# Weighing the values with the values as the stationary operand, in column halves, and one reduction for both heads' largest scores

## What is computed

```
q, k = rope(x @ wq.T + bq, x @ wk.T + bk)          # 16 heads of 64, 512 tokens
s = q @ k.T / sqrt(64), causal                     # per head, 512 x 512
p = exp(s - max(s))                                # kept undivided
o = (p @ v) / sum(p) + bv                          # v without its bias
out = concat(o over heads) @ wo.T + bo
```

## Time and profile before

| | us |
|---|---|
| median of 3 executions | 2499.45 (2493.75 to 2513.72) |
| the profiled execution | 2502.42 |
| its span on the core | 2500.5 |
| what lies around the span | 1.92 |

### The profile page before, as it was taken

The page is one execution under the profiler, slowest core; times in us unless marked ns, Lnnn a source line. Parts: engine busy times, 40 slices in busy tenths (PEclk is TensorE's granted clock), DMA queues, the critical chain, the costliest instruction groups (busy, mean ns, idle before and its releaser), DMA issues.

```text
span 2500.5 us, 38952 instructions
## 1 busy us (share of the span) xinstructions
PE 2057.5 (82%) x11640; PEld 1430.8 (57%) x11640; DVE 1680.5 (67%) x2937; ACT 1187.7 (47%) x2702; POOL 951.3 (38%) x581
## 2 busy tenths in 40 slices
PE   4147788998899888998889878998889988989985
PEld 1013366665567556665566556665566655666764
DVE  2975678558965798558865788558876588645431
ACT  1214366345643466345653456344663456424631
POOL 0330366106920386106930277104850077203501
PEclk9558789999999999999999989998999998999997
DMA  2000002231123212231113212231123211142233
GB/s 103 0 0 17 17 35 71 91 109 43 57 70 113 69 51 74 90 110 40 61 64 119 68 42 84 67 106 56 43 68 116 85 45 55 65 133 71 71 105 116
DMA packets 82452, 175.06 MB, mean 70 GB/s; under 512 B 11448, under 2 KB 42560, under 8 KB 81984
## 3 DMA queue, kind: packets, MB, share of 16 engines
q1 hardware_dynamic: 78144, 164.05, 19.0%
q0 software_dynamic: 4096, 8.40, 1.1%
HBM read 123.71 MB, written 15.14 MB: 56 GB/s over the span
## 4 chain that ended last, share of the span: by engine, by line
PE 50%; DVE 22%; issue 14%; ACT 6%; POOL 4%; DMA 3%; SPq 1%; DVEq 0%; ACTq 0%; POOLq 0%
PE G L1065 7%; DVE HS L1542 7%; PE G L1050 5%; PE FM L1039 3%; PE FC L1027 3%; PE G L943 3%; PE G L954 3%; PE G L937 3%; ACT REG L1347 2%; DMA MW<-moe 2%; PE G L1082 2%; PE FM L907 2%; DVE maxes L1843 2%; DVE HC L1564 2%; PE FM L749 2%
## 5 line engine op out<-in xcount | busy, mean ns | idle before, releaser
L1542 DVE TENSOR_TENSOR_SCAN HS<-DA,D 128x1024 f32<-128x1024 f32 x128 | 374.8, 2928 | 20.5 <-ACT DA L1224 19.9
L1065 PEld LDWEIGHTS G<-REG 128*128 128x128 f32 x2560 | 350.4, 199 | 60.6 <-issue 50.2
L1065 PE MATMUL G<-REG 128*128 128x64 f32 x2560 | 358.6, 273 | 3.2 <-DVE REG L1855 3.2
L1967 POOL TENSOR_TENSOR Y<-Y,HC 128x1024 f32<-128x1024 f32 x114 | 269.1, 2361 | 181.3 <-DVE HC L1564 180.3
L1050 PE MATMUL G<-ident,REG 128*128 128x128 f32 x1280 | 242.1, 289 | 116.3 <-ACT REG L1347 114.0
L1347 ACT ACTIVATE REG<-G 128x128 f32<-128x128 f32 (+3 forms) x512 | 223.4, 436 | 121.4 <-PE G L1050 117.0
L1978 POOL TENSOR_TENSOR REG<-REG,cos_t 128x512 f32<-128x512 f32 x128 | 170.4, 1331 | 264.2 <-ACT REG L1323 264.1
L1050 PEld LDWEIGHTS G<-ident,REG 128*128 128x128 f32 x1280 | 149.0, 150 | 166.1 <-issue 132.6
L1339 ACT ACTIVATE REG<-G,maxes 128x128 f32<-128x128 f32 (+3 forms) x384 | 195.6, 510 | 81.9 <-DVE maxes L1843 81.9
L1981 POOL TENSOR_TENSOR REG<-REG 128x512 f32<-128x512 f32 x128 | 204.2, 1596 | 57.4 <-DMA REG<-ROT 48.8
L1039 PE MATMUL G<-REG 64*128 64x128 f32 (+3 forms) x768 | 217.8, 481 | 8.4 <-POOL REG L1981 7.4
(11 more groups left out here) (290 smaller groups left out, 4272.4 us busy)
## 6 DMA issues: line engine op xcount, KB each, us to landing
MW<-moe SPq DMA_DIRECT2D x120, 768.0 KB, 4.2
REG<-ROT SPq DMA_DIRECT2D x256, 128.0 KB
EW<-experts SPq DMA_DIRECT2D x16, 514.5 KB, 4.7
XG<-x_rows SPq DMA_DIRECT2D x8, 960.0 KB, 5.4
y_rows<-YO SPq DMA_DIRECT2D x120, 64.0 KB, 1.5
X<-xT SPq DMA_DIRECT2D x8, 256.0 KB, 6.1
W<-weights SPq DMA_DIRECT2D x1, 2048.0 KB, 9.5
REG<-xT SPq DMA_DIRECT2D x8, 256.0 KB, 3.2
```

The source lines that it names most:

```text
L1065: mm = pe.matmul(G[3][:, col:col + DK], PT[:, n % 2, c * P:(c + 1) * P], V[:, c, j * P + h * DK:j * P + (h + 1) * DK], start=c == 0, stop= ...
L1542: dve.tensor_tensor_scan(HS[:, :, :].rearrange("p h s -> p (h s)"), DA[:, n % 2, :, :].rearrange("p h s -> p (h s)"), D1[:, :, :].rearrang ...
L1967: pool.tensor_tensor(Y[:, :, :], Y[:, :, :], HC_EARLY if early else HC[:, n % 2, :, :], ALU.add).then_inc(y_add.sem, 1)
```

## The change

`weigh_values` now takes both heads of a step together. V is the stationary operand (64 columns) and PT moves (128 columns), so the result comes out turned: head 0 on partitions 0 to 63 of G3 and head 1 on partitions 64 to 127. `turn_out` is gone. ACT copies G3 into O when a pair is done. The reciprocals can no longer be applied along partitions, so PE spreads them over the bank FC with eight small products (`spread_inverse`), and DVE multiplies O by that bank straight into the slot. The bias bv goes through wo once, at the start, and is added to bo. G1 with G0 and FM with G4 are now two tensors of two banks each, and `largest` reduces both heads of a step in one instruction. `front(0)` on POOL has a new wait.

```
...
+        SCORES = [ctx.enter_context(nc.psum_tensor(n, [P, 2, S], F32)) for n in ("G1_G0", "FM_G4")]
...
             if t_ == OUT_STEP and j_:
-                guest[s_] = (("out", j_ - 1), (ot_copy, j_))
+                guest[s_] = (("out", j_ - 1), (o_d, j_))
...
-            def weigh_values(b, n):
-                pe.wait_ge(pt_copy.sem, pt_copy.at(b, n + 1))
...
-                col = t * P + h * DK
                 for c in range(t + 1):
-                    mm = pe.matmul(G[3][:, col:col + DK], PT[:, n % 2, c * P:(c + 1) * P],
-                                   V[:, c, j * P + h * DK:j * P + (h + 1) * DK], start=c == 0, stop=c == t)
+            def weigh_values(b, s):
+                pe.wait_ge(pt_copy.sem, pt_copy.at(b, 2 * s + 2))
...
+                    for h in range(2):
+                        mm = pe.matmul(G[3][h * DK:(h + 1) * DK, t * P:(t + 1) * P], V[:, c, j * P + h * DK:j * P + (h + 1) * DK],
+                                       PT[:, h, c * P:(c + 1) * P], start=c == 0, stop=c == t)
...
+            def spread_inverse(b, j):
+                pe.wait_ge(rec_d.sem, rec_d.at(b, j + 1))
                 bank = take(b, ("out", j))
                 for t in range(TILES):
-                    mm = pe.transpose(bank[:, t * P:(t + 1) * P], O[:, t * P:(t + 1) * P], ident[:, :])
-                mm.then_inc(ot_mm.sem, 1)
+                    for h in range(2):
+                        mm = pe.matmul(bank[h * DK:(h + 1) * DK, t * P:(t + 1) * P],
+                                       rows[:, j % 2, 1, h * TILES + t:h * TILES + t + 1].to_broadcast([P, DK]), ident[:, :],
+                                       start=True, stop=True)
+                mm.then_inc(rinv_mm.sem, 1)
...
                     turn(b, 2 * s)
-                    if s:
-                        weigh_values(b, 2 * s - 1)
...
                     elif key[0] == "out":
-                        turn_out(b, key[1])
+                        spread_inverse(b, key[1])
...
-                    if t_ == 0 and s + 2 < STEPS:
+                    if s + 2 < STEPS:
                         scores(b, s + 2)
-                    weigh_values(b, 2 * s)
-                    if t_ and s + 2 < STEPS:
-                        scores(b, s + 2)
-                weigh_values(b, N_TILES - 1)
+                    weigh_values(b, s)
+                spread_inverse(b, PAIRS - 1)
                 for j in range(PAIRS - 1):
                     project_out(b, j)
-                turn_out(b, PAIRS - 1)
...
             def copy_out(b, j):
...
-                act.wait_ge(ot_mm.sem, ot_mm.at(b, j + 1))
-                act.activation(ot_slot(j), ring_bank[("out", j)][:, :], ACT.Identity, bias=vec("bv", j)).then_inc(ot_copy.sem, 1)
+                act.wait_ge(pv_mm.sem, pv_mm.at(b, PER_PAIR * (j + 1)))
+                act.activation(O, G[3][:, :], ACT.Copy).then_inc(o_copy.sem, 1)
...
                     copy_turned(b, 2 * s)
+                    if s and s % TILES == 0:
+                        copy_out(b, s // TILES - 1)
...
+            def largest(b, s):
+                dve.wait_ge(sc_mm.sem, sc_mm.at(b, 2 * s + 2))
+                dve.tensor_reduce(maxes[:, j % 2, :].rearrange("p (h t) -> p h t", h=2)[:, :, t], SCORES[s % 2][:, :, 0:(t + 1) * P], AX.X, ALU.max,
                                   negate=True).then_inc(nm_d.sem, 1)
...
+                dve.wait_ge(o_copy.sem, o_copy.at(b, j + 1))
+                dve.wait_ge(rinv_mm.sem, rinv_mm.at(b, j + 1))
+                dve.tensor_tensor(ot_slot(j), O, ring_bank["out", j][:, :], ALU.mult).then_inc(o_d.sem, 1)
...
                     if key[0] == "proj":
                         rotate(b, key[1])
+                    elif key[0] == "out":
+                        divide(b, key[1])
...
                 for n in range(STATES):
+                    if n + 1 < STATES:
+                        pool.wait_ge(scan_d.sem, scan_d.at(b, n + 2))
+                        pool.sem_inc(pool_passed, 1)
                     front_step(b, n)
```

More of the change, by code:

```diff
@@ L235, in build @@
         y_rows = nc.dram_tensor("y_rows", (MOE_TILES * MOE_ROWS, D), F32).ap()
-        FB, FC, FM = (ctx.enter_context(nc.psum_tensor(n, [P, S], F32)) for n in ("FB", "FC", "FM"))
-        G = [ctx.enter_context(nc.psum_tensor(f"G{k}", [P, S], F32)) for k in range(5)]
+        FB, FC = (ctx.enter_context(nc.psum_tensor(n, [P, S], F32)) for n in ("FB", "FC"))
+        SCORES = [ctx.enter_context(nc.psum_tensor(n, [P, 2, S], F32)) for n in ("G1_G0", "FM_G4")]
+        FM = SCORES[1][:, 0, :]
+        G = [SCORES[0][:, 1, :], SCORES[0][:, 0, :], *(ctx.enter_context(nc.psum_tensor(f"G{k}", [P, S], F32)) for k in (2, 3)), SCORES[1][:, 1, :]]
         n_loads, n_late = 16 * 10, 16 * 3
@@ L328, in build @@
         o_d = signal("o_d", PAIRS)
-        ot_mm = signal("ot_mm", PAIRS)
-        ot_copy = signal("ot_copy", PAIRS)
+        rinv_mm = signal("rinv_mm", PAIRS)
+        o_copy = signal("o_copy", PAIRS)
         wo_mm = signal("wo_mm", PAIRS)
@@ L1164, in late @@
                 pe.wait_ge(s_late, n_late)
-                pe.wait_ge(s_made, 17)
+                for j in range(PAIRS):
+                    mm = pe.matmul(G[2][:, 0:1], w("wo", j * D), vec("bv", j), start=j == 0, stop=j == PAIRS - 1)
+                mm.then_inc(s_bv, 1)
+                pe.wait_ge(s_made, 18)
             def finish(t):
@@ L1394, in phase_2 @@
                         add_bias(b, key[1])
-                    elif key[0] == "out":
-                        copy_out(b, key[1])
                     elif key[0] == "turn":
@@ L1881, in phase_2 @@
                 largest(b, 0)
-                largest(b, 1)
                 if f is not None:
@@ L1888, in phase_2 @@
                     if s + 1 < STEPS:
-                        largest(b, 2 * s + 2)
-                        largest(b, 2 * s + 3)
+                        largest(b, s + 1)
                     if t_ == 0 and j:
-                        divide(b, j - 1)
+                        invert_sums(b, j - 1)
                     if s == 1:
@@ L1923, in late @@
                 dve.tensor_scalar(q_b, q_b, DK ** -0.5, None, ALU.mult).then_inc(s_made, 1)
-                dve.wait_ge(s_made, 17)
+                dve.wait_ge(s_bv, 1)
+                dve.tensor_tensor(vec("bo"), vec("bo"), G[2][:, 0:1], ALU.add).then_inc(s_made, 1)
+                dve.wait_ge(s_made, 18)
             def finish(t):
```

56 lines of the change are left out of this document (23 added, 33 removed).

## The result

The changed kernel takes 2555.07 us (median of 4 executions, 2545.25 to 2562.72), beside 2496.6 us before (4 executions). The ratio is 1.0214 with a 95% interval of 1.0179 to 1.0248: slower, by about 2%. The forecast was 2545 us, 1.8% slower. The profiled execution has a span of 2559.7 us, 59.2 more than before.

What follows compares the result with a forecast made beforehand. PE was taken to bound sequence 7, and PE and DVE, both nearly full, the sequences with a front. 2502.4 + 11 + 49 - 15 = 2547 us, 2545 as median, 1.8% slower; range 2475 to 2620 us.

Steps and rivals of the forecast that it cites:

- The wait that loses its cover: On PE, moving the weighing opens ACT's copy round trip, 0.62 to 0.95 us; a pair of heads gets 1.4 us longer.
- The wait in a window of the steps: Sign: the wait of PE's transposes for ACT's copy rises from 16 us to over 25.
- The weighing, and its surcharge: On PE, overlapping column halves take (t + 1) * 0.214 us for a step, plus 0.2 us for each group.
- Rival 3: PE's column halves do not overlap, 0.107 us an instruction: 2625 us or more; chance 0.10.
- Sequence 7, +11 us: Last sequence, no front beside it, PE bounds: 8 pairs at 1.4 us more, 11 us (3 to 14).
- Sequences 0 to 6, +49 us: Sequences with a front: PE's row 6, ACT's waits 3.3, bank 1.8, less 2.6; 7 us each (2 to 12).
- the reduction: On DVE, one for two heads saves 2.6 us a sequence; the first head's later maximum costs 3.3 us.
- The bank FC: DVE's later multiplication frees it late, so PE's projection waits: 1.8 us a sequence.
- One thing more: the scans beside POOL's gathers: They make sequences 4 to 6 6 us longer than 1 to 3; shifted steps could turn any: 20 us either way.
- The front of sequence 0, -15 us: POOL's new wait keeps additions off DVE's scans, about 1.1 us for each of 15: -15 us (-10 to -17).
- Rivals 1 and 2: DVE's load hides PE's longer row beside the front: 2490 us (chance 0.22), or faster, 2454 to 2470 us (0.13).
- rival 2: PE's open round trip hidden in over 25 of 32 steps, sequences 4 to 6 at 132 us: 2454 to 2470; chance 0.13.

Runs made afterwards that it cites:

- e1: Changed kernel with both heads' weighing of the previous step put between the two transposing groups, and a third slot for the turned scores: 2485.5 us.
- e4: Kernel before with only the order changed, both weighings of a step behind the scores and none between the transposing groups: 2570.7 us.
- e6: Kernel before with the banks paired and one reduction for both heads of a step, nothing else: 2541.2 us.
- e7: Changed kernel with the spread of the reciprocals and DVE's multiplication moved from t = 1 to t = 0: 2547.7 us.
- e5: Kernel before with only POOL's new wait in the front of sequence 0: 2481.4 us.
- e11: Changed kernel with both heads' weighing between the transposing groups, a third copy slot, and one reduction for each head: 2463.5 us.
- e9: Kernel before, old products and two reductions, with the front's wait, a third copy slot and both heads' weighing between the transposing groups: 2492.3 us.
- e12: Changed kernel with useless transposes on PE at steps 1, 11 and 23 in laps with a front: 2514.5 us.
- e2: Changed kernel with all blocks of head 0 weighed first, then all of head 1, instead of in turn: 2561.3 us.

## Why the prediction was right, step by step

- *The wait that loses its cover.* Right, and the largest term. The round trip at t = 3 was put at 0.95 us and stands open at 2396.13 to 2396.90 as PE's idle of 0.78; counted as in the prediction, from 0.45 us behind the first transpose (2395.92), it is 0.98. The wait in a window of the steps was to pass 25 us and came to 23.9 in the steps (24.7 with the 12 us ahead of them), a little short of it. e1 and e4 show the cause from both sides, 19 and 18 us in sequence 7. In the laps, where I had 6 us for PE's row, e4 adds 4.2 us each by work with the cover alone. e1 takes 7.7 off ((920.7 - 867.0) / 7), but with more cover than there was before.
- *The weighing, and its surcharge.* Right. A step was put at (t + 1) * 0.214 + 0.2 us, 1.06 at t = 3; measured 1.03, and 0.81, 0.59 and 0.37 for the others (put at 0.84, 0.63, 0.41). The spread was put at 1.06 and took 1.02 us. Rival 3 (no overlap) is out. That loading held the old form is read from this: in the kernel before, from 2347.16, the loads of the eight products start 0.112 us apart and take 0.192 us each, so they leave no gap, and 64 moving columns take as long (0.105 us) as the 128 of a transpose (0.11).
- *Sequence 7, +11 us.* Too small: it was +16.5, outside my 3 to 14, and the steps take 122.6 us, not 117. The pair was put at +1.4 us; it is +1.7 in most (13.71 to 15.38), 13 us for eight. Half clock at the start of the sequence, of which there was none before, is 1.7 us: the clock is 0.84, 0.50 and 0.81 in the three windows of 2 us from 2333. The rest lies in single steps of the first three pairs, which I had priced like the others.
- *Sequences 0 to 6, +49 us.* The sum was +51.3, and the agreement is partly luck. I had 7 us for each lap, 12 at most; measured are -3.0 for sequence 0, +11.6 to +13.8 for 1 to 3, +0.6 for 4, and +7.3 to +7.5 for 5 and 6. By work it is +40.6 in all, 5.8 a lap; 10.6 us are half clock, which I had no term for. Within the work, the reduction was put at +0.7 us a lap (3.3 for the first head, -2.6 for the fixed part). By the table four pairs of runs give 2.7, 1.6, 1.7 and 0.1, by span times clock 23, 7, 18 and 18 us in the whole kernel: some 1 to 3 us a lap, so it was put too low. The reason that I gave, a longer wait of ACT for the largest scores, shows in e6 (23.8 us against 14.7) and not in the changed kernel (6.9). The saving of DVE's time itself was right: the groups of L1847 come to 210.0 us against 235.7 for L1843, 3.2 us a sequence. The bank FC (1.8 us) was wrong: 2.5 us in the whole kernel, and with that wait gone (e7) the laps' work does not fall.
- *"One thing more: the scans beside POOL's gathers."* Half right. I saw that sequences 4 to 6 were 6 us longer and allowed 20 us for a flip of laps. The scans are longer there (40.6 us in the steps against 34.5), though DVE's busy time is the same (117 us in both). The long one at step 8 meets POOL's additions and multiplications; beside a gather of 2.87 us (623.91) the same scan took its 2.28. Flips did come: they make most of e6, and sequences 1 to 3 of the changed kernel grew the most (in sequence 1 the scans take 39.4 us in place of 34.5). What my reasoning lacked is the clock, which makes some 5 of the 6 us.
- *The front of sequence 0, -15 us.* Right: -16.7 alone (e5), -13.7 up to the first turn in the changed kernel.
- *Rivals 1 and 2, DVE covers it.* They did not come: DVE is busy for 114 of the 145 us now, and the laps got longer. What came nearest to rival 2 is e1, where the open round trip is closed again.
- *The range.* 2475 to 2620 held. For the edit of e6 alone the same sum gave no more than 10 us, and it cost 45.

What stays open: which part of the new form lets the laps of e11 keep the clock where e9 loses it, and whether filler on top of e11 gains again. Neither was tried. Nor do the parts add up: the order alone costs 74 us, the one reduction alone 45, and the front's wait gains 14, which makes 105, where the change costs 58. So no part has a price of its own in the laps with a front.

## What to carry to other kernels

An instruction that stands between two uses of one buffer may be worth more as cover than it costs; before it is moved, the round trip that it hides has to be read from the timeline and put into the sum. When windows that run the same list differ in length, multiply each by its mean granted clock before explaining anything: if the products agree, most of the difference is clock. What made PE idle ahead of it still has to be looked up in the timeline; here it was also a scan that took 5.55 us in place of 2.28. And where PE waits 2 to 3 us in a place that cannot be cured, useless products there can pay, as they did in e12 (2514.5 us against 2555.1).

## What the runs showed of the hardware

- Filler of 24 transposes (2.79 us, e12) in an idle place kept the granted clock at 1.00; without it, in the changed kernel, 2.81 us of idle were followed by a mean of 0.59 over 4 us, with a projection at nearly double its time (1.92 against 1.02 us). Three such places a lap were worth 54 us of half clock in seven laps.
- In the kernel before, a scan on DVE took 2.28 us beside a gather of POOL of 2.87 us, and 5.55 us where it ran into two of POOL's additions and multiplications in a row.
- Column halves overlap even when all products of one half stand ahead of those of the other, but then only in part: 16 in 1.51 us (e2), against 1.03 turn about (the changed kernel; one by one would be 1.71, worked out from 0.107 us each); up to 8 there is no difference.
- Every group of column halves in the changed kernel has some 0.17 us around its streams (16 in 1.03 us, 0.86 of it streams). For the row halves of the scores it is near that: four products of 256 columns take 0.64 us (2398.32 to 2398.96), 0.43 of it streams.
